# Stencil kernel: when GpSimd enters the first stencil steps, where two products read the field, and where the first half's tail lies in the second half's start

## The reference

```python
    g  = relu(bn(dwconv(h, wg)));  g1 = relu(bn(dwconv(h, wg1)));  gy, gx = sobel(h)
    Dx = 1 / (gy*gy/4 + 1);        Dy = 1 / (gx*gx/4 + 1)
    E  = (ux + vy) * DT            # from shifted g and g1
    D  = 1 / (1 + 2*Bx + 2*By)     # Bx, By = Dx*DT, Dy*DT
    for _ in range(5):
        prev = h
        h = D * (c0*h0 - 2*E*h + cm_x*roll(h, 1, 2) + cp_x*roll(h, -1, 2) + cm_y*roll(h, 1, 3) + cp_y*roll(h, -1, 3))
        h = h + D * (2*DT) * fsrc
        h0 = prev
```

## Time and profile before

| | |
|---|---|
| Runs of the kernel before | 912.39, 911.88, 911.01 us; median 911.88 |
| The profiled execution | 911.18 us, of which span 909.2 us |
| Mean granted TensorE clock | 0.957 |
| VectorE busy | 802.6 us, 88% of the span |
| TensorE busy | 734.8 us, 81% |
| ScalarE busy | 560.2 us, 62% |
| GpSimd busy | 527.1 us, 58% |

### The profile page before, as it was taken

The page is one execution under the profiler, slowest core; times in us unless marked ns, Lnnn a source line. Parts: engine busy times, 40 slices in busy tenths (PEclk is TensorE's granted clock), DMA queues, the critical chain, the costliest instruction groups (busy, mean ns, idle before and its releaser), DMA issues.

```text
span 909.2 us, 10555 instructions
## 1 busy us (share of the span) xinstructions
PE 734.8 (81%) x3866; PEld 499.9 (55%) x3866; DVE 802.6 (88%) x682; ACT 560.2 (62%) x960; POOL 527.1 (58%) x243
## 2 busy tenths in 40 slices
PE   3895999877667788788799889988766677888896
PEld 2342344344466777678655434435446566787783
DVE  6979997769999998999969899775999999989984
ACT  2962242227849898979486723313585987897942
POOL 3105899020479698778510479911127978878851
PEclk9999899999799899999989899999989999999999
DMA  3002000000445455455200120000033455545431
GB/s 113 1 24 69 0 1 0 0 1 0 140 151 174 142 190 191 139 186 179 77 1 0 59 58 0 0 1 0 1 98 120 148 177 173 201 153 182 160 110 23
DMA packets 34065, 78.18 MB, mean 86 GB/s; under 512 B 15704, under 2 KB 15840, under 8 KB 34016
## 3 DMA queue, kind: packets, MB, share of 16 engines
q1 hardware_dynamic: 32608, 76.23, 25.1%
q0 software_dynamic: 320, 1.05, 0.5%
q10 hardware_dynamic: 1088, 0.26, 0.1%
HBM read 70.71 MB, written 2.62 MB: 81 GB/s over the span
## 4 chain that ended last, share of the span: by engine, by line
DVE 35%; PE 29%; ACT 16%; issue 16%; POOL 2%; DMA 0%; DVEq 0%; POOLq 0%; SPq 0%; ACTq 0%
ACT arena L957 13%; PE ps L748 7%; DVE arena L1773 7%; PE ps L509 6%; DVE ps L1764 6%; PE ps L548 4%; DVE HS L1773 3%; DVE arena L1728 3%; PE ps L762 2%; PE ps L640 1%; ACT ps L957 1%; PE ps L662 1%; DVE arena L1748 1%; DVE arena L1667 1%; DVE arena L1646 1%
## 5 line engine op out<-in xcount | busy, mean ns | idle before, releaser
L396 POOL TENSOR_TENSOR arena<-arena 128x1024 f32<-128x1024 f32 x85 | 200.5, 2368 | 59.8 <-DVE arena L1773 54.6
L957 ACT ACTIVATE arena<-arena 128x128 f32<-128x128 f32 (+3 forms) x412 | 157.0, 455 | 86.9 <-DVE arena L1667 67.7
L1773 DVE TENSOR_TENSOR_SCAN arena<-arena,ps 128x1024 f32<-128x1024 f32 x86 | 194.6, 2276 | 9.7 <-ACT arena L957 5.5
L957 ACT ACTIVATE arena<-arena,Amat 128x1024 f32<-128x1024 f32 x128 | 143.0, 1141 | 7.2 <-DVE arena L1773 6.0
L640 PE MATMUL ps<-mat,arena 128*128 128x128 f32 x1016 | 136.6, 279 | 5.6 <-POOL arena L396 5.2
L599 PE MATMUL ps<-mat,arena 128*128 128x128 f32 x560 | 81.6, 294 | 64.4 <-DVE arena L1773 36.9
L640 PEld LDWEIGHTS ps<-mat,arena 128*128 128x128 f32 x1016 | 118.4, 145 | 9.8 <-POOL arena L396 7.9
L748 PE MATMUL ps<-arena,mat 128*128 128x512 f32 x240 | 110.9, 615 | 14.4 <-DVE arena L1643 14.4
L396 POOL TENSOR_TENSOR arena<-HS,arena 128x1024 f32<-128x1024 f32 x42 | 100.1, 2382 | 29.7 <-DVE HS L1773 27.0
L599 PEld LDWEIGHTS ps<-mat,arena 128*128 128x128 f32 x560 | 65.8, 146 | 79.4 <-DVE arena L1773 46.8
L957 ACT ACTIVATE arena<-ps 128x1024 f32<-128x1024 f32 (+2 forms) x55 | 46.1, 849 | 87.2 <-PE ps L486 45.4
(11 more groups left out here) (219 smaller groups left out, 1340.3 us busy)
## 6 DMA issues: line engine op xcount, KB each, us to landing
arena<-c_rows SPq DMA_DIRECT2D x128, 512.0 KB, 3.8
arena<-arena SPq DMA_DIRECT2D x16, 252.0 KB
out<-arena SPq DMA_DIRECT2D x28, 64.0 KB, 2.3
xres<-x POOLq DMA_DIRECT2D x4, 256.0 KB, 5.2
xres<-x SPq DMA_DIRECT2D x4, 256.0 KB, 4.1
convw<-conv_w SPq DMA_DIRECT2D x1, 576.0 KB
c_rows<-ROWS SPq DMA_DIRECT2D x4, 128.0 KB, 1.9
mat<-mats SPq DMA_DIRECT2D x1, 448.0 KB, 3.5
```

The source lines that it names most:

```text
L396: tt(HC[s % 2], HS[s % 3], CB[s % 4], ALU.mult).then_inc(S("hc"), 1)
L957: return nc.scalar.activation(out_, in_, func, bias=bias, scale=scale, accum_out=accum_out)
L1773: nc.vector.tensor_tensor_scan(HS[s % 3], DA[s % 3], PS[q][:, :], 0.0, ALU.mult, ALU.add).then_inc(S("scan"), 1)
```

## The change

It has five parts. GpSimd's `first_two_sources` waits for the first `x_neighbours` instead of the second `times_D`, and its loop of triples starts after both images' `x_neighbours`, by one wait ahead of the loop. `last_first_sources` and `last_source` read the field in `PS[3]` instead of `fz`, with a wait for `field(1)`. In the second half, `F[1]["X3"]` moves to the tile `sden`, and the wait for `final` moves from `y_neighbours` to the second of the first `products` of image 1. VectorE's order changes in the second half. ScalarE's `from_D(h, 0)` goes behind `reciprocal`, `small_group_shift` and `scale`, and `copy_out` goes behind `field(0)` and `first_seed(0)`.

```diff
@@ -130,10 +130,11 @@
         for name, at in [("SQ", ("DL", 1)), ("XN", ("DU", 0)), ("V1", ("DU", 1)), ("X3", ("XS", 0)),
                          ("T1", ("XS", 1)), ("A2", ("DL", 0)), ("T2", ("DL", 1)), ("OT", None)]:
             F[0][name] = D[0][at[0]][:, at[1] * L:at[1] * L + L] if at else D[0]["R1"]
-        for name, at in [("SQ", "W3"), ("XN", "R1"), ("V1", "W2"), ("X3", "W4"), ("T1", "W3"), ("A2", "W2"),
+        for name, at in [("SQ", "W3"), ("XN", "R1"), ("V1", "W2"), ("T1", "W3"), ("A2", "W2"),
                          ("T2", "R1")]:
             F[1][name] = D[1][at]
         F[1]["OT"] = A[1]["fr"][:, 0:L]
+        F[1]["X3"] = A[1]["sden"]
 
         UU = [D[0]["W4"], D[0]["W5"], D[1]["W4"], D[1]["W5"]]
         DA = [D[0]["W0"], D[0]["W1"], D[1]["DA2"]]
@@ -404,7 +405,7 @@
             def first_two_sources(h):
                 a = A[0]
                 pool.wait_ge(S("a_P0"), 2 * h + 1)
-                pool.wait_ge(S("a0_G"), 2 * h + 2)
+                pool.wait_ge(S("a_Pm"), 2 * h + 1)
                 pool.wait_ge(S("a_div"), 2 * h + 1)
                 tt(img(a["g"]), img(a["X"]), frm(a["fz"])[:, 1:33, 1:33], ALU.mult).then_inc(S("a0_g"), 1)
 
@@ -430,13 +431,13 @@
                     root(D[1], h - 1, 3, 1)
                 first_two_sources(h)
                 source(h, 0)
+                pool.wait_ge(S("a_Pm"), 2 * h + 2)
                 with pool.Fori(0, STEPS) as t:
                     for k in range(2):
                         a, it = A[k], STEPS * h + t
                         hw = wrapped(a["hw"])
 
                         pool.wait_ge(S("a_Q6"), 2 * h + k + 1)
-                        pool.wait_ge(S("a_Pm"), 2 * h + k + 1)
                         pool.wait_ge(S(f"a{k}_act"), 3 * it + 1)
                         tt(img(a["R"]), img(a["Pmx"]), hw[:, :, 0:32], ALU.mult)
                         tt(img(a["XY"]), img(a["G"]), hw[:, :, 2:34], ALU.mult).then_inc(S(f"a{k}_x"), 1)
@@ -1265,13 +1266,12 @@
                     small_group_var(D[1], h - 1, 3, 1)
                     squares(h, 1)
                     copy_x3(h - 1, 1)
-                    from_D(h, 0)
                     reciprocal(h, 1)
                     small_group_shift(D[1], h - 1, 3, 1)
                     scale(h - 1, 1)
+                    from_D(h, 0)
                     relu(h, 1, 1)
                     copy_a2(h - 1, 1)
-                    copy_out(h - 1, 1)
                 if h == 0:
                     relu(h, 1, 1)
                     from_D(h, 1)
@@ -1285,6 +1285,7 @@
                     act.wait_ge(S("a_Pe"), 2 * h + k + 1)
                     first_seed(h, k)
                     if h > 0 and k == 0:
+                        copy_out(h - 1, 1)
                         from_D(h, 1)
                 for k in range(2):
                     wrap(h, k, 1)
@@ -1609,12 +1610,10 @@
             def last_source(h):
                 a = A[1]
                 dve.wait_ge(S("a_D"), 2 * h + 2)
-                stt(img(a["Sc"]), img(a["Dc"]), 2 * DT, frm(a["fz"])[:, 1:33, 1:33], ALU.mult, ALU.mult).then_inc(S("a_Sc1"), 1)
+                stt(img(a["Sc"]), img(a["Dc"]), 2 * DT, img(PS[3]), ALU.mult, ALU.mult).then_inc(S("a_Sc1"), 1)
 
             def y_neighbours(h, k):
                 a = A[k]
-                if h > 0 and k == 1:
-                    dve.wait_ge(S("final"), 2 * h)
                 dve.wait_ge(S("a_K"), 2 * h + k + 1)
                 dve.wait_ge(S(f"a{k}_G"), 2 * h + 1)
                 tt(a["Pmy"], a["Ky"], a["G1"], ALU.subtract).then_inc(S("a_Py"), 1)
@@ -1641,6 +1640,8 @@
                 if t == 0:
                     dve.wait_ge(S(f"a{k}_g"), 4 * h + 1)
                 tt(img(a["Pmy"]), img(a["Y"]), field, ALU.mult).then_inc(S(f"a{k}_c"), 1)
+                if h > 0 and k == 1 and t == 0:
+                    dve.wait_ge(S("final"), 2 * h)
                 tt(img(a["sden"]), img(a["Ky"]), field, ALU.mult).then_inc(S(f"a{k}_c"), 1)
                 dve.wait_ge(S("a_Pe"), 2 * h + k + 1)
                 tt(img(a["X"]), img(a["Pe"]), field, ALU.mult).then_inc(S(f"a{k}_e"), 1)
@@ -1658,7 +1659,8 @@
                 dve.wait_ge(S("a_P0"), 2 * h + 2)
                 dve.wait_ge(S("a_div"), 2 * h + 2)
                 dve.wait_ge(S("a1_G"), 2 * h + 2)
-                tt(img(a["g"]), img(a["X"]), frm(a["fz"])[:, 1:33, 1:33], ALU.mult).then_inc(S("a1_g"), 1)
+                dve.wait_ge(S("a1_act"), 3 * STEPS * h + 2)
+                tt(img(a["g"]), img(a["X"]), img(PS[3]), ALU.mult).then_inc(S("a1_g"), 1)
 
             def new_h(h, k, t):
                 a = A[k]
@@ -1825,16 +1827,16 @@
                     times_D(h, 0, 1)
                     y_neighbours(h, 0)
                     x_neighbours(h, 0)
+                    minus_E(h, 0)
                     fractions_D(h, 1)
-                    minus_E(h, 0)
                     times_D(h, 1, 0)
                     fractions_K(h, 1)
                     y_neighbours(h, 1)
+                    times_D(h, 1, 1)
+                    x_neighbours(h, 1)
                     products(h, 0, 0)
                     minus_E(h, 1)
-                    times_D(h, 1, 1)
                     last_first_sources(h)
-                    x_neighbours(h, 1)
                     products(h, 1, 0)
                     last_source(h)
                 if h == 0:
```

## The result

The changed kernel takes 899.85 us as a median of four runs (899.02 to 900.84), against 912.13 us for the kernel before (911.01 to 912.44). The ratio is 0.9865, with a 95% interval of 0.9849 to 0.988: 12.3 us faster, where 11.7 were forecast and 900.2 named. The profiled execution took 899.3 us, with a span of 897.5.

The account below looks back on a forecast made before the run. VectorE's stalls beside GpSimd delay each half's first `new_h`, behind which TensorE's 57 us are fixed. Gains of 7.2 + 4.5 = 11.7 us take the median from 911.88 to 900.2 us; range 898.0 to 905.6.

Parts of the forecast that it names:

- First half, 7.2 us: First half's stencil: stalls of 8.0 us go, a 0.6 us wait for `field(1)` comes, `new_h(0,0)` 7.2 us earlier.
- T: End of `x_neighbours(1)` on VectorE, after which GpSimd's triples start; forecast 82.7 in the first half, 522.0 in the second.
- Second half, 4.5 us: Second half's stencil, schedule redone: `last_first_sources` starts at 527.4, `new_h(0,0)` comes at 533.3, 4.5 us earlier.
- the two held instructions: Second half, VectorE: `times_D(1,0)` held until GpSimd's `first_two_sources` ends at 512.9, `y_neighbours(1)` until `source` ends at 516.3.
- The rival itself: TensorE still at 1.2 GHz in second half's `divergence(1)`, 12.2 us instead of 6.1; gain 6.4, 905.5 us; chance 0.07.
- Reading PSUM: `last_first_sources` and `last_source` on VectorE: priced at nothing by the rows; the skill page's estimate was 0.26 us less gain.
- GpSimd's reserve: End of each half's steps: GpSimd's ten triples end 0.5 us (first half) and 0.7 us (second) ahead of TensorE.
- it doesn't bind: First half's end: GpSimd finishes at 150.4, TensorE at 150.9, so GpSimd does not set the end.
- with nobody waiting for GpSimd: Sign for the new trace: TensorE's ends near 150.9 and 590.4, no engine waiting for GpSimd.
- the slower rival: GpSimd held 2.8 us a triple by products and `new_h` sets both halves' ends; four each: 921.3 us; chance 0.03.
- `copy_out` was not held up: Rival, second half: `copy_out` behind `first_seed(0)` delayed to 526.3, `new_h(0,0)` 1.8 later; gain 5.4, 906.5 us; chance 0.07.
- no other cause: Rival, first half: four long VectorE instructions not due to GpSimd, only second half's 4.5 left; 907.7 us; chance 0.06.

Follow-up runs that it names:

- e1: The kernel before with only GpSimd's waits of the change added: 913.68 us, ratio 1.0017.
- e3: The changed kernel with `last_first_sources` and `last_source` reading the SBUF tile again: 903.09 us, ratio 0.9908.
- e2: The changed kernel with GpSimd's waits put back as before: 911.23 us, ratio 1.0004.
- e9: The changed kernel measured once more, unchanged: 900.43 us, ratio 0.9882.
- e6: The changed kernel with the first product of GpSimd's first triple made twice in each half: 904.21 us, ratio 0.9916.
- e7: The changed kernel with ScalarE's `field(k)` ahead of the wait for the roll at step 0: 903.36 us, ratio 0.9902.

## Why the prediction was right

**First half, 7.2 us: measured 7.23.** Each step can be read off. The four held instructions are gone (T 8.02 earlier; 8.0 forecast). `new_h` came 7.28 earlier; the difference is the wait for `field(1)`, 0.66 measured, 0.6 forecast, behind a roll of 8.6 (8.7). TensorE's stretch behind the first `new_h` is 56.95 against 56.90. e1 and e3 split the gain: the waits alone bring 5.4 us of it, and the PSUM reads the other 1.8.

**Second half, 4.5 us: measured 4.64.** T was forecast at 522.0 on the old clock; it is 515.56 + 497.74 - 491.65 = 521.65. The wait for `copy_a2`, the two held instructions and the wait for `field(1)` are where they were expected, and `new_h` came 4.65 earlier. Some of that closeness is luck: the first half of `y_neighbours(1)` was out 0.5 us before the forecast 517.5, and the roll took 9.05 us instead of 8.8. e2 and e1 show that the gain needs both the waits and something of the rest, and e3 that the PSUM reads are 1.65 of it. That VectorE's order is the main part of the rest is read from T in e1, 34.19 against 23.91; no run undid this order alone.

**The clock.** I had `final` at 518.2 in the times of the profile before, with TensorE as slow in `keep_x3` and `second_dct` as it was there. In the first profile of the changed kernel it had its full clock, and `final` came at 509.67 + 6.09 = 515.8. In e9, the same kernel, it had not, and `final` came at 518.4. The end was the same in both, so this step did no harm either way. The rival itself, that the lower clock still stands in `divergence(1)`, did not happen: in both profiles the clock was back at 1.00 before it.

**Reading PSUM.** L1663 takes 1.22 us from PSUM; L1661 took 1.21 from SBUF. The 0.065 us for each, an estimate from the Trainium skill, page VectorE: DVE Perf Modes, section on the TRN2 errata, is not there. I had priced the part at nothing, which is its price for VectorE; e3 shows what it gives: 3.4 us, through GpSimd. It was in the forecast only as the absence of a hold: the ten triples at 6.77 us each take it for granted.

**GpSimd's reserve.** I had 0.5 and 0.7 us. Between the ends of the last rows it is 150.96 against 151.16, and 583.80 against 584.22, so 0.2 and 0.4. But the end waits for L1491, which GpSimd's last instruction holds, and by that it is nothing and 0.2; e6 (0.0 and 0.1) and e7 (0.02 and 0.21) agree. A part of what is missing is at the start: the first triple begins 83.36 - 83.03 = 0.33 and 516.18 - 515.56 = 0.62 behind T, where I had taken it as immediate. The step "it doesn't bind" thus held by luck as much as by the sum: in the first half GpSimd and TensorE end together, and against the sign "with nobody waiting for GpSimd" two late `new_h` wait for it there, by 0.57 and 0.64. That GpSimd can set the end, as in the slower rival, e1, e3 and e6 show; its condition, a hold in the later triples, was not met.

**The other rivals.** `copy_out` was not held up: it started at 509.71, with nothing but `final` before it. The long instructions of the first half had no other cause: e2 has them back with the waits alone undone. The Trainium skill, page SBUF — State Buffer, section on who interferes with whom, says that a VectorE instruction with two SBUF inputs contends with a GpSimd instruction that reads SBUF, and that the ports they share are an exclusive lock. The held pairs shown here fit: a VectorE 1.22 becomes 3.4 at most, a GpSimd 2.2 becomes 3.2, and L1491's 0.22 becomes 1.32.
